# Issuing the weight loads of the wide cross attention in the norm block ahead of it

## The reference

```python
x = _layernorm(x + _L0_attn_ref(x, ...))
x = _layernorm(x + _L0_xattn_ref(x, ctx, ctx, ...))
x = _layernorm(x + _L0_ffn_ref(x, ...))
x = _layernorm(x + _L1_attn_ref(x, ...))          # 16 heads of 64
x = _layernorm(x + _L1_xattn_ref(x, ctx, ...))    # 16 heads of 64, 77 keys
x = _layernorm(x + _L1_ffn_ref(x, ...))
```

```python
q = jnp.einsum('bqm,mhd->bqhd', inputs_q, Wq) + bq
k = jnp.einsum('bkm,mhd->bkhd', inputs_kv, Wk) + bk
v = jnp.einsum('bkm,mhd->bkhd', inputs_kv, Wv) + bv
attn = softmax(einsum('bqhd,bkhd->bhqk', q / sqrt(64), k))
out = jnp.einsum('bhqk,bkhd->bqhd', attn, v)
return jnp.einsum('bqhd,hdm->bqm', out, Wo) + bo
```

## Time and profile before

| | |
|---|---|
| median of 3 runs | 2275.23 us |
| lowest and highest | 2266.92 and 2277.47 us |
| the profiled execution | 2271.61 us |
| its span, first to last instruction | 2269.9 us |
| mean granted clock of TensorE | 0.897 of full speed |
| closing norm of the wide self-attention | 1856.16 to 1871.82 us |
| first product of the operand block | 1882.29 us |

### The profile page before, as it was taken

The page is one execution under the profiler, slowest core; times in us unless marked ns, Lnnn a source line. Parts: engine busy times, 40 slices in busy tenths (PEclk is TensorE's granted clock), DMA queues, the critical chain, the costliest instruction groups (busy, mean ns, idle before and its releaser), DMA issues. The chain is left out here.

```text
span 2269.9 us, 33575 instructions
## 1 busy us (share of the span) xinstructions
PE 1775.7 (78%) x9665; PEld 1000.7 (44%) x9718; DVE 1384.8 (61%) x4754; ACT 1032.5 (45%) x1970; POOL 155.7 (7%) x281
## 2 busy tenths in 40 slices
PE   4177775584149668699994999999999977997997
PEld 2144443353013223367772444444444434665664
DVE  7388885565358557433335777777777763774445
ACT  3288881362016446433331555656665543332221
POOL 2000003001000000100002000000000001330000
PEclk7599996696659889889996999999999987998999
DMA  1543200510540330010001000000000001000000
GB/s 57 80 44 38 29 0 11 79 25 7 89 51 5 39 41 2 3 38 19 19 10 37 1 1 1 1 1 1 1 0 1 1 1 39 1 1 21 17 19 26
DMA packets 57636, 48.74 MB, mean 21 GB/s; under 512 B 12691, under 2 KB 53047, under 8 KB 57527
## 3 DMA queue, kind: packets, MB, share of 16 engines
q1 hardware_dynamic: 57527, 47.45, 13.0%
HBM read 38.30 MB, written 8.91 MB: 21 GB/s over the span
## 5 line engine op out<-in xcount | busy, mean ns | idle before, releaser
L1432 PE MATMUL ps_s<-d_KZ,d_Q 128*128 128x512 f32 x512 | 265.4, 601 | 16.1 <-issue 6.8
L1580 ACT ACTIVATE d_PR<-d_PR,d_NM 128x512 f32<-128x512 f32 x256 | 184.7, 721 | 189.9 <-DVE d_NM L1511 189.5
L557 DVE TENSOR_REDUCE c_NM<-ps_t 128x1 f32<-128x512 f32 x256 | 169.9, 688 | 96.7 <-PE ps_t L437 95.0
L1507 DVE CUSTOM_DVE_ANT_0 d_PR<-ps_s,d_BH 128x512 f32<-128x512 f32 x256 | 176.2, 688 | 61.5 <-PE ps_t L1440 44.7
L437 PE MATMUL ps_t<-KX,QX 96*128 (+1 forms) x256 | 107.6, 425 | 105.1 <-DVE c_IB L575 47.6
L2288 DVE SCALAR_TENSOR_TENSOR X<-ps_t,GATE,X 128x128 f32<-128x128 f32 x272 | 76.7, 344 | 185.1 <-PE ps_t L2213 185.1
L619 ACT ACTIVATE c_PT<-ps_s 128x1024 f32<-128x1024 f32 x128 | 130.4, 1024 | 126.2 <-PE ps_s L460 124.3
L1440 PEld LDWEIGHTS ps_t<-ident,d_PR 128*128 128x128 f32 x1024 | 121.3, 141 | 150.8 <-issue 132.6
L1587 ACT ACTIVATE d_PT<-ps_t 128x512 f32<-128x512 f32 x256 | 149.9, 586 | 50.6 <-PE ps_t L1440 49.0
L762 ACT ACTIVATE a_PR<-a_PR,a_NM 128x128 f32<-128x128 f32 (+3 forms) x256 | 129.8, 555 | 78.0 <-DVE a_NM L743 78.0
L1440 PE MATMUL ps_t<-ident,d_PR 128*128 128x128 f32 x1024 | 156.4, 275 | 10.1 <-ACT d_PT L1587 8.1
(11 more groups left out here) (330 smaller groups left out, 3118.2 us busy)
## 6 DMA issues: line engine op xcount, KB each, us to landing
QX<-split_parts SPq DMA_DIRECT2D x108, 128.0 KB
KX<-split_parts SPq DMA_DIRECT2D x72, 128.0 KB
f_W<-in_L_ffn_w SPq DMA_DIRECT2D x16, 256.0 KB, 3.1
split_parts<-a_PARTS SPq DMA_DIRECT2D x8, 384.0 KB, 10.3
split_parts<-c_PARTS SPq DMA_DIRECT2D x8, 384.0 KB, 11.0
g_W<-in_L_ffn_w SPq DMA_DIRECT2D x24, 128.0 KB, 2.2
split_parts<-b_PARTS SPq DMA_DIRECT2D x4, 384.0 KB, 10.7
X<-in_x SPq DMA_DIRECT2D x4, 256.0 KB
```

The lines of the kernel that those rows point to most:

```text
L557: nc.vector.tensor_reduce(NM[:, qt, j:j + 1], c.ps_t[:, i % 2, :], AX.X, ALU.max, negate=True).then_inc(maxed, 1)
L1432: nc.tensor.matmul(c.ps_s[:, qt % 2, :], Q[:, p % 2, qt * P:(qt + 1) * P], KZ[:, p % 2, i % 2, :], start=True, stop=True).then_inc(scores, 1)
L1507: nc.vector.tensor_tensor_reduce(out=PR[:, h % 2, qt, :], in0=c.ps_s[:, qt % 2, :], in1=BH[:, h, S - P - qt * P:2 * S - P - qt * P], scale ...
L1580: nc.scalar.activation(PR[:, h % 2, qt, :], PR[:, h % 2, qt, :], ACT.Exp, bias=NM[:, h % 2, qt:qt + 1], accum_out=DEN[:, h % 2, qt:qt + 1] ...
```

## The change

The seven tiles move out of `wide_operands` into an object `WideWeights`, made in `decoder` before `finish` and kept until the end of the cross attention, together with OT. Its `load` issues the same seven transfers in the same order, on the same engine, with one semaphore. `finish` gets an argument `early`, called first on its SP list. `wide_operands` keeps its waits for that semaphore and issues no loads. The tiles of the cross attention now share one `ExitStack` with OT, so they lie at other addresses.

```diff
-def finish(c, tag, source, wo=None, bias=None, mode="post", pre=None, out=None, OT=None):
+def finish(c, tag, source, wo=None, bias=None, mode="post", pre=None, out=None, OT=None, early=None):
...
             @block.sync
             def _(sp):
+                if early is not None:
+                    early(sp)
                 if wo is not None:
...
+class WideWeights:
+
+
+    def __init__(self, c, tag, ctx):
+        self.WQ, self.WK, self.WV = (c.sb(f"{tag}_W{n}", [P, H * HD64], F32, ctx) for n in "qkv")
+        self.WO = c.sb(f"{tag}_Wo", [P, PAIRS, P], F32, ctx)
+        self.BQ, self.BK, self.BV = (c.sb(f"{tag}_B{n}", [P, PAIRS], F32, ctx) for n in "qkv")
+        self.loaded = c.sem(f"{tag}_ow")
+
+    def load(self, sp, wq, bq, wk, bk, wv, bv, wo):
+        for dst, src in ((self.WK, wk), (self.WV, wv), (self.WQ, wq)):
+            sp.dma_start(dst[:, :], src.rearrange("m h d -> m (h d)")).then_inc(self.loaded, 16)
+        sp.dma_start(self.WO[:, :, :], wo.rearrange("(g e) d n -> (e d) g n", e=2)).then_inc(self.loaded, 16)
+        for dst, src in ((self.BQ, bq), (self.BK, bk), (self.BV, bv)):
+            sp.dma_start(dst[:, :], src.rearrange("(g e) d -> (e d) g", e=2),
+                         allow_slow_non_contiguous=True).then_inc(self.loaded, 16)
...
             @block.sync
             def _(sp):
-                for dst, src in ((WK, wk), (WV, wv), (WQ, wq)):
-                    sp.dma_start(dst[:, :], src.rearrange("m h d -> m (h d)")).then_inc(s_w, 16)
-                sp.dma_start(WO[:, :, :], wo.rearrange("(g e) d n -> (e d) g n", e=2)).then_inc(s_w, 16)
-                for dst, src in ((BQ, bq), (BK, bk), (BV, bv)):
-                    sp.dma_start(dst[:, :], pairs(src), allow_slow_non_contiguous=True).then_inc(s_w, 16)
                 sp.wait_ge(s_split, SPLIT_OPS + 1)
...
             wide_self_attention(c, "d", a["L1_attn_Wq"], a["L1_attn_Wk"], a["L1_attn_Wv"], a["L1_attn_Wo"], OT)
-            finish(c, "d", "dm", OT=OT)
-
-        with ExitStack() as own:
+            weights = WideWeights(c, "e", own)
+            finish(c, "d", "dm", OT=OT, early=lambda sp: weights.load(
+                sp, *(a[f"L1_xattn_{n}"] for n in ("Wq", "bq", "Wk", "bk", "Wv", "bv", "Wo"))))
             A, CP, U = flat_operand_tiles(c, "e", own)
-            wide_operands(c, "e", *(a[f"L1_xattn_{n}"] for n in ("Wq", "bq", "Wk", "bk", "Wv", "bv", "Wo")), A, CP, U)
+            wide_operands(c, "e", weights, A, CP, U)
             flat_cross(c, "e", A, CP, U, a["L1_xattn_bo"])
```

More of the change, by code:

```diff
@@ L1636, in flat_operand_tiles, with wide_operands @@
     return A, CP, U
-def wide_operands(c, tag, wq, bq, wk, bk, wv, bv, wo, A, CP, U):
+class WideWeights:
[11 more added lines that the diff above has]
+                         allow_slow_non_contiguous=True).then_inc(self.loaded, 16)
+def wide_operands(c, tag, weights, A, CP, U):
     nc = c.nc
     with ExitStack() as own:
-        WQ, WK, WV = (c.sb(f"{tag}_W{n}", [P, H * HD64], F32, own) for n in "qkv")
-        WO = c.sb(f"{tag}_Wo", [P, PAIRS, P], F32, own)
-        BQ, BK, BV = (c.sb(f"{tag}_B{n}", [P, PAIRS], F32, own) for n in "qkv")
+        WQ, WK, WV, WO = weights.WQ, weights.WK, weights.WV, weights.WO
+        BQ, BK, BV, s_w = weights.BQ, weights.BK, weights.BV, weights.loaded
         BQH = c.sb(f"{tag}_BQH", [P, PAIRS * H], F32, own)
@@ L1654, in wide_operands @@
         CH = c.sb(f"{tag}_CH", [H, NPART, B * KC], BF16, own)
-        (s_w, s_zero, s_bq, s_k, s_v, s_wqt, s_kout, s_vout, s_wqtout, s_a, s_u, s_aout, s_uout, s_c, s_split, s_cp,
+        (s_zero, s_bq, s_k, s_v, s_wqt, s_kout, s_vout, s_wqtout, s_a, s_u, s_aout, s_uout, s_c, s_split, s_cp,
          s_t, s_tout) = (
             c.sem(f"{tag}_o{n}") for n in
-            ("w", "zero", "bq", "k", "v", "wqt", "kout", "vout", "wqtout", "a", "u", "aout", "uout", "c", "split", "cp",
+            ("zero", "bq", "k", "v", "wqt", "kout", "vout", "wqtout", "a", "u", "aout", "uout", "c", "split", "cp",
              "t", "tout"))
@@ L1661, in wide_operands @@
         W = CHUNKS * P
-        pairs = lambda ap: ap.rearrange("(g e) d -> (e d) g", e=2)
         def scored(h):
```

## The result

| | before | changed |
|---|---|---|
| median of 7 runs | 2271.74 us | 2259.82 us |
| lowest and highest | 2266.92 and 2280.39 | 2255.84 and 2264.42 |
| profiled execution: span | 2269.9 us | 2262.7 us |
| norm's first transpose to first product of the operand block | 26.10 us | 15.82 us |

The time fell to 0.9945 of before, with a 95% interval of 0.9926 to 0.9964, that is by 12.5 us (8 to 17). The changed kernel was timed again with the experiments, with 12 runs beside 35 of before: 0.9953 (0.9933 to 0.9972), 10.7 us. The forecast was a gain of 10.2 us, 0.9955.

A forecast was written before the change was run, and what follows sets the result against it. It took the bound at the operand block's start to be a bare 10.2 us wait for seven loads. Hiding 10.19 us, with 0 for traffic, refills and clock, took the 2275.23 us median to 2265.1 us; range 2257 to 2272.

The forecast's parts named there:

- steps 1 and 2: Loads issued at the closing norm's start; operand block's first product 0.28 us after the norm's last work, gaining 10.19 us.
- The margin of the cover: In the closing norm: last load lands at 1866.3 us, norm lasts until 1871.82, so 5.5 us are left over.
- step 3: In the norm: 2 MB of transfers cost VectorE at most 0.9 us; 0 taken.
- step 4: In the norm: instruction refills meeting the weights cost between 0 and 1.6 us; 0 taken.
- step 5: TensorE's clock in the operand block: no change taken, with 2.2 us to win or 6.6 us to lose.
- C: Rival, chance 0.13: full clock at operand block's first product, one low cross-attention step less; 4.3 us more gained, 2260.8 us.
- rival D: Rival, chance 0.04: cross attention stays at half clock, 2.07 us more per half tile; 2287.9 us with 11 more steps.

The follow-up runs named there:

- the tiles alone: Against before: the seven tiles reserved early at the changed kernel's addresses, loads still issued at the start of the operand block; ratio 0.9999.
- second run: The changed kernel, unaltered, timed and profiled again with the experiments; ratio to before 0.9953.

## Why the prediction was right

**Where the wait came from and that it goes (steps 1 and 2).** Right, and shown by the tiles alone (26.10 us, nothing gained) against the changed kernel (15.82 and 15.86). The boundary was put at 0.28 us from one row; it measured 0.30 and 0.31. The term of the sum was 10.19 us and measured 10.28, of which 0.12 are a slightly shorter norm. So close a hit is in part luck, since the norm alone varies by 0.4 us.

**The margin of the cover.** 5.5 us were forecast, 5 us measured, since the last landing took 3.4 us instead of 3.0 and the issues 8.63 instead of 8.39. The run with more traffic shows what happens beyond it.

**The traffic in the norm (step 3).** The value taken, none, was right to what the clock leaves to be seen, and the bound of 0.9 us was not needed: 15.20 us with and without 2 MB at the like clock, 15.36 us at 366 GB/s.

**The refills (step 4).** None taken, none seen: they took about the same time, and the first product stood 0.30 us behind the boundary, with no bytes on any queue from the end of the loads to 1880 us. So nothing was fetched there that the old wait had covered. The Trainium skill (Runtime: NRT & Kernel Launch, section Instruction fetch mechanics) warns of a taken branch out of what is held; whether this boundary has one, no run here shows. By the rule of the Trainium skill on arbitration (DMA: Bandwidth & Descriptors, section on queues, rings and completion order) a refill waits for a packet and not for all weights. The trace agrees: the DMA view of 1860 to 1862 us has the first refill, with 3.5% of 16 engines or 1.1 us, and the weights and biases went on until 1869.4. Between loads on the same queue no such turn-taking shows: the 5.8 us of the two small vectors.

**The clock (step 5, rivals C and D).** In the operand block nothing changed, as forecast: the mean of 0.53 in 1879 to 1880 puts the rise at 1879.94, 4.8 us after the first product, where before had 4.65. That it came so close is luck in part: in the eleven profiles the rise comes 3.8 to 6.1 us after the first product.

In the cross attention the mechanism was there and both sizes were off. C put one step less at 2.07 us. The changed kernel was low there only from 1917.48 to 1927.72, 10.2 us instead of 17.1, and its 32 half tiles took as long (117.2 and 117.3 us); with 6.8 us low they took 115.6 (second run). Over all profiles with the bias where it was, 17.1 us low gave 117.1 to 117.3, 13.7 gave 116.1, 10.2 gave 116.9 and 117.2, and 6.8 gave 115.5 and 115.6: at most 1.8 us for 10 us of low clock, and not in order. What counts is which steps the low time meets. Here are the step from the fourth maximum to the fifth in before, and then the two steps up to the fifth in the changed kernel:

```profile
1930.52:1936.15 5.63, 5.63 (x22) 4.17 (x22) 2.50 (x4) 1.31 (x2) 1.22 (x1) 0.63 0.01 3
```

```profile
1915.64:1922.63 6.99, 4.45 (x12) 2.27 (x12) 2.46 (x5) 1.31 (x2) 3.70 (x4) 0.63 0.00 0
1922.63:1928.61 5.98, 5.98 (x22) 4.32 (x23) 2.50 (x5) 1.31 (x2) 1.21 (x1) 0.57 0.01 3
```

The first steps are the pipeline filling, with 6 to 12 records of TensorE instead of 22. Before's first two took 3.39 us each at the low clock; in the changed kernel they took 1.9 and 2.5 us at the full one, but its third step, the one of 6.99 us, gave most of that back, and the three together took 11.8 and 11.4 us. In the 6.99 us TensorE was busy for 4.45 only; GpSimd's adds are behind a part of it, since with the output bias early the three steps took 9.8 us, where the second run of the changed kernel has 11.3. The step up to the fifth maximum is the first with all of TensorE's work, and TensorE is busy for the whole of it. Its excess over 3.56 us goes with the low time in it: 2.07 us for 4.2 us low in before, 2.42 for 5.1 in the changed kernel, and 0.48 to 0.51 us for each us in all eleven profiles. All later steps, at the full clock, took the same time in every profile (96.3 to 96.4 us from the sixth maximum to the last).

So rival D's price, 2.07 us for each of 32 steps, was read from a step that was low for three quarters only, and it was too small. By the half us for each us, a step wholly at the low clock would take about 7 us, some 3.4 us more (an estimate; no trace has such a step), and three of them would have used up the gain, not five. What kept D away is that the clock of the cross attention rose in each of the eleven profiles, after 17.1 us at the most. The rows of before did not show that it had to.

**The numbers.** The forecast of 2265.1 us was made from the median of three runs, 2275.23; seven runs put before at 2271.74, and 10.2 off that is 2261.5, against 2259.82 measured. Of the 5.3 us by which the median missed the forecast 3.5 thus lie in the base; the range had room for them. I gave 0.54 to "within 0.5%" and 0.42 to "faster". The ratios of the two measurements, 0.9945 and 0.9953, lie on either side of that line, so it was about even, as the text had it.

## What to carry over

When a block begins with a wait for loads that depend on nothing computed, find the block before it in which the DMA queue is idle and measure two lengths: from first issue to last landing, and how long that block lasts. If the first is the shorter, the whole wait goes, down to what is late next: here the boundary, in the self-attention VectorE's table. If it is the longer, only the overrun stays. But put the loads behind whatever the hiding block itself waits for, since one queue serves them in order.

Price a move like this from marks inside the trace (norm start to first product), not from the span: here the span of single executions moved by 16 us for causes 650 us earlier, and the way from the norm's start to the first product, in two profiles of one kernel, by 0.04 us, with up to 0.4 us more where the clock meets the norm otherwise.

## What the runs showed of the hardware

- The issue time of a transfer on SP is for a good part the state of the queue: for the key bias 0.58 us on an empty queue and 3.14 or 4.53 us behind 2 MB, for the query bias 0.38 us on an empty queue and 8.35 us behind 6 MB. The value bias took 0.57 and 1.40 us in two runs without weights ahead of it, and why it did is open.
- TensorE at half the clock cost half a us for each us of it where TensorE was busy throughout (0.48 to 0.51 in eleven profiles). A stage as a whole lost less: 17.1 us low instead of 6.8 made the 32 half tiles 1.8 us longer at most.
- Loads of 366 GB/s into SBUF left VectorE's 52 instructions of the norm at 11.75 us (11.76 without traffic).
- Around the start of the last block, the experts, the clock was low for 17.1 us in all in five of the eleven profiles, and for 20.5 us, in two pieces, in the other six. From the first expert load to the end it took 216.1 to 216.5 us in the five and 217.5 to 218.2 in the six. In the second run of the changed kernel this gave back all that the short low time in the cross attention had brought: 387.58 us from the first product to the end, 387.57 in before. That the one leads to the other is not shown: the run with the self-attention's weights had the second piece too, with a cross attention no faster than before.
